# One load of the decoder weights over 128 partitions, gathers issued step by step, and a split of the last pair of chunks: an AdaLN and FFN kernel on one core

## The reference, cut to what matters

```python
# layer 0: a conditioned input, then a top-2 mixture of 8 experts
U   = mu @ W_dec + b_dec            # (128, 64) @ (64, 129 * 30): per sequence a 128 x 30 matrix and 30 offsets
t   = x @ U[:, :128*30] + U[:, 128*30:]   # 30 numbers per token
x0  = t @ V                         # then gate (softmax of the top 2 of 8), experts: gelu(x0 W1 + b1) W2 + b2
x   = x + ffn0(x0)
# layer 1: layer norms, table rows gathered by token id, an integrating MLP, then a ternary FFN
x   = x + ffn1(cond(x, ids, states))
# ffn1: h = silu(a1 x) * (a2 x); h = gelu(h1 h); h = gelu(h2 h); w3 h
```

## Time and profile before

| | us |
|---|---|
| median of 3 runs | 443.49 |
| lowest and highest of 3 runs | 441.01, 443.49 |
| the profiled execution, its own time | 443.04 |
| its span, first to last instruction | 441.2 |
| mean granted TensorE clock in it | 0.978 |

### The profile page before, as it was taken

How to read it: one execution, slowest core, us unless ns; L and a number is a source line. 1 busy time by engine, 2 the same in 40 slices (tenths; PEclk the granted TensorE clock), 3 DMA queues, 4 the chain that set the end, 5 groups by cost and what they waited for, 6 DMA issues and landing times.

```text
span 441.2 us, 5719 instructions
## 1 busy us (share of the span) xinstructions
PE 416.0 (94%) x1804; PEld 272.6 (62%) x1804; DVE 315.6 (72%) x651; ACT 290.7 (66%) x515; POOL 142.8 (32%) x129
## 2 busy tenths in 40 slices
PE   4888998999999999999999999999999997999994
PEld 2856544554656765677567665776577646687773
DVE  2889998887985776766886577596784687656542
ACT  1568775797937766497647763975678455776563
POOL 3016896663631650273028261317211012010000
PEclk9799996999999999999999999999999998999999
DMA  8975564473352352532315245035501100000000
GB/s 242 364 293 161 179 174 119 112 229 68 104 155 51 71 163 97 118 99 73 111 40 159 75 116 150 0 70 181 134 3 49 46 3 0 1 0 25 0 25 27
DMA packets 29961, 45.08 MB, mean 102 GB/s; under 512 B 3461, under 2 KB 22378, under 8 KB 29418
## 3 DMA queue, kind: packets, MB, share of 16 engines
q1 hardware_dynamic: 25440, 32.33, 25.7%
q0 software_dynamic: 3584, 10.49, 7.1%
q10 hardware_dynamic: 906, 1.87, 1.5%
HBM read 40.67 MB, written 4.03 MB: 101 GB/s over the span
## 4 chain that ended last, share of the span: by engine, by line
PE 79%; DVE 8%; ACT 5%; issue 3%; DMA 2%; POOL 2%; another core or an unknown queue 1%; ACTq 0%; POOLq 0%; DVEq 0%
PE bank L644 23%; PE bank L746 20%; PE bank L692 7%; PE bank L636 6%; PE bank L782 6%; PE bank L731 5%; PE bank L823 2%; PE bank L660 2%; DMA muT<-cond_512T_in 2%; PE bank L699 2%; PE bank L771 2%; POOL rstd L1446 1%; ACT mG L890 1%; ACT YN L895 1%
## 5 line engine op out<-in xcount | busy, mean ns | idle before, releaser
L644 PE MATMUL bank<-mG,W 128*128 128x512 f32 x256 | 121.3, 604 | 0.1
L890 ACT ACTIVATE mG<-bank,keepP 128x512 f32<-128x512 f32 x128 | 85.3, 685 | 32.2 <-PE bank L636 30.2
L1446 POOL TENSOR_TENSOR rstd<-ve,mhalf 128x4 f32<-128x4 f32 x24 | 34.0, 1419 | 173.0 <-DVE ve L1196 172.1
L1181 DVE TENSOR_TENSOR mG<-mG,gwbs 128x1024 f32<-128x1024 f32 x64 | 77.1, 1220 | 8.8 <-ACT mG L890 4.4
L644 PEld LDWEIGHTS bank<-mG,W 128*128 128x128 f32 x256 | 48.4, 194 | 44.2 <-issue 39.9
L636 PE MATMUL bank<-ts,A 96*128 96x512 f32 x128 | 66.8, 553 | 1.3 <-ACT mG L890 1.1
L955 ACT ACTIVATE G<-bank,keepP 128x512 f32<-128x512 f32 x48 | 32.8, 696 | 25.4 <-PE bank L746 20.1
L1427 POOL DMA_INDIRECT gp<-pgb_in,ixall x32 | 36.8, 1149 | 27.4 <-DVE norms L1233 17.7
L1430 POOL DMA_INDIRECT gcm<-ctm,ixcm x32 | 36.5, 1140 | 9.8 <-issue 9.8
L746 PE MATMUL bank<-hA_h,h1w_h 128*128 128x512 f32 x96 | 38.9, 405 | 0.0
L746 PE MATMUL bank<-hA_l,h1w_h 128*128 128x512 f32 x96 | 38.6, 402 | 0.0
(11 more groups left out here) (241 smaller groups left out, 804.3 us busy)
## 6 DMA issues: line engine op xcount, KB each, us to landing
gwbs<-gate_w SPq DMA_DIRECT2D x32, 512.0 KB
keep<-xT_in SPq DMA_DIRECT2D x8, 256.0 KB, 5.8
outT<-keep SPq DMA_DIRECT2D x8, 256.0 KB, 2.0
t_split<-tsS SPq DMA_DIRECT2D x7, 192.0 KB
ts<-t_split SPq DMA_DIRECT2D x7, 192.0 KB
W1T<-W1T_in SPq DMA_DIRECT2D x1, 1024.0 KB, 9.4
W<-W2T_in SPq DMA_DIRECT2D x1, 1024.0 KB, 13.8
hs<-h1T_in SPq DMA_DIRECT2D x1, 1024.0 KB, 6.5
```

Source lines behind the costliest of these rows:

```text
L644: mm = pe.matmul(OACC[:, :], W2[:, e * HC + c, :], mG[n % NMG][:, c, :], start=False, stop=(e == E - 1 and c == HC - 1))
L890: act.activation(mG[e % NMG][:, c % HC, :], HM[n % 2][:, :], ACT.Gelu, bias=b1c[:, c:c + 1]).then_inc(m_gelu, 1)
L1181: dve.tensor_tensor(mine, mine, gate.unsqueeze(1).broadcast_to([P, HC, TT, P]), ALU.mult).then_inc(m_q, 1)
L1446: step(pool.tensor_tensor(rstd[:, n, :], ve[:, n, :], mhalf[:, :], ALU.pow))
```

## The change

Three things are changed. First, `W_dec` is loaded by one transfer from SP's queue into `Wd`, over all 128 partitions: its source is seen as two halves h of columns (outermost), 64 rows m and 1920 numbers c. The lower partitions now carry features 0 to 63. The 30 last columns, `wd_u`, are a transfer of their own from ACT's queue, into a place in `gap`; `ld_wd` still counts four transfers. ACT issues `muT` first, then `wd_u`, `bdec`, `V`, `keepP`, `earlyP` and `bdec_u`. The last piece of `Wp` goes from DVE to ACT, and `sq_()` with the two products behind it is moved on DVE from ahead of the additions to behind the copies of G8, just ahead of `tb0`. POOL's two memsets count one each on `wp_zero`, and all wait for 2. Second, the step `tab` of POOL becomes four steps `tab0` to `tab3`, each with the waits of `tab` ahead of its two indirect transfers; in `ORDER` the four follow one another where `tab` was. Third, in the last FFN chunks 10 and 11 (the last two ahead of the last product) get their high and low parts one at a time.

```diff
-        Wd = sb("Wd", [P, KR * (DH + 1)], stack=early)
+        Wd = sb("Wd", [P, KR * DH], stack=early)
...
-        bdec_u = gap[0:KR, KA + KR:KA + KR + 1]
+        wd_u = gap[0:MU, KA + KR:KA + 2 * KR]
+        bdec_u = gap[0:KR, KA + 2 * KR:KA + 2 * KR + 1]
...
-        PIECES = ("v", "v", "v", "a", "v", "a", "v", "v")
+        PIECES = ("v", "v", "v", "a", "v", "a", "v", "a")
...
+        def alone(j, k):
+
+            return j is TAIL["p"] and k >= 3 * FC - 2
+
         def tail_lo(eng, j, k):
 
-            eng.wait_ge(p_lo[j.s], j.n * (FC + 4) + (k + 1 if k < FC else FC + (k - FC) // 2 + 1))
+            eng.wait_ge(p_lo[j.s], k + 1 if k < FC else FC + (k - FC) // 2 + 1 + (alone(j, k) and k % 2))
...
-                    "fgp9 fhp8 fgp10 fgp11 fhp10"),
+                    "fgp9 fhp8 fgp10 fgp11 fhp10 fhp11"),
...
-                    "flp6 -for flp8 flp10 fop"),
+                    "flp6 -for flp8 flp10 flp11 fop"),
...
-                (0, "tcl0 tcl1 tcl2 srt ix tcl3 tab tcl4 tcl5 rt0 tcl6 tcl7 rt1"),
+                (0, "tcl0 tcl1 tcl2 srt ix tcl3 tab0 tab1 tab2 tab3 tcl4 tcl5 rt0 tcl6 tcl7 rt1"),
...
-            load(Wd[0:MU, :], A["W_dec"][:, KR * DH:KR * (D + 1)], ld_wd)
+            load(Wd[:, :], A["W_dec"][:, 0:KR * D].rearrange("m (h c) -> h m c", h=2), ld_wd)
...
-            load(Wd[MU:P, 0:KR * DH], A["W_dec"][:, 0:KR * DH], ld_wd)
             for at in (0, MU):
                 load(muT[at:at + MU, :], A["cond_512T"], ld_wd)
+            load(wd_u, A["W_dec"][:, KR * D:KR * (D + 1)], ld_wd)
+            load(bdec, A["b_dec"][:, 0:KR * D].rearrange("o (i k) -> (o i) k", k=KR), ld_bd)
             load(Vk[:, :], A["V"], ld_v)
             load(keepP[:, :], A["keepP"], ld_v)
-            load(bdec, A["b_dec"][:, 0:KR * D].rearrange("o (i k) -> (o i) k", k=KR), ld_bd)
...
-            sq_()
-            step(dve.tensor_scalar(hs1[:, :], fsc[:, 0:FC], 0.5, None, ALU.mult))
-            dve.tensor_tensor(cs12[:, :], hs1[:, :], fsc[:, FC:2 * FC], ALU.mult)
...
             ins.then_inc(g8_ready, 1)
+            sq_()
+            step(dve.tensor_scalar(hs1[:, :], fsc[:, 0:FC], 0.5, None, ALU.mult))
+            dve.tensor_tensor(cs12[:, :], hs1[:, :], fsc[:, FC:2 * FC], ALU.mult)
             run(steps, ORDER["DVE"])
...
-            def tables(b):
+            def tables(b, t):
...
-                for t in range(TT):
-                    j = b * TT + t
+                j = b * TT + t
```

More of the change, by code:

```diff
@@ L164, in build @@
         Wp = hs[:, 0:KR * D].rearrange("m (k i) -> m k i", k=KR)
-        wd = [Wd[0:MU, :].rearrange("m (i k) -> m k i", k=KR), Wd[MU:P, 0:KR * DH].rearrange("m (i k) -> m k i", k=KR)]
-        wd_u = Wd[0:MU, KR * DH:KR * (DH + 1)]
-        turned_wd = [Wp[0:MU, :, DH:D], Wp[MU:P, :, 0:DH]]
+        halves = (slice(0, MU), slice(0, DH)), (slice(MU, P), slice(DH, D))
+        wd = [Wd[rows, :].rearrange("m (i k) -> m k i", k=KR) for rows, _ in halves]
+        turned_wd = [Wp[rows, :, cols] for rows, cols in halves]
         warmA = sb("warmA", [2, P], stack=early)
@@ L1003, in fh_tail @@
                     return
-                act.wait_ge(p_g[j.s], j.n * 2 * FC + k - FC + 2)
+                w = 1 if alone(j, k) else 2
+                act.wait_ge(p_g[j.s], k - FC + w)
                 dst = hB if k < 2 * FC else hC
-                act.activation(dst[0][:, c:c + 2, j.cols], j.G[:, c:c + 2, j.cols], ACT.Copy).then_inc(p_hi[j.s], 1)
+                act.activation(dst[0][:, c:c + w, j.cols], j.G[:, c:c + w, j.cols], ACT.Copy).then_inc(p_hi[j.s], 1)
             def low_check(n):
@@ L1075, in _ @@
             act.wait_ge(ld_wd, 64)
-            act.wait_ge(wp_zero, 1)
+            act.wait_ge(wp_zero, 2)
             for q in range(8):
@@ L1079, in _ @@
                     mine = slice(4 * q, min(4 * q + 4, KR))
-                    act.activation(turned_wd[1][:, mine, :], wd[1][:, mine, :], ACT.Copy)
-                    act.activation(turned_wd[0][:, mine, :], wd[0][:, mine, 0:DH], ACT.Copy).then_inc(wd_act, 1)
+                    act.activation(turned_wd[0][:, mine, :], wd[0][:, mine, :], ACT.Copy)
+                    act.activation(turned_wd[1][:, mine, :], wd[1][:, mine, :], ACT.Copy).then_inc(wd_act, 1)
             load(w12s[:, :], A["w12T"], ld_w[0])
@@ L1288, in fl_tail @@
                 else:
-                    dst, w = (hB if k < 2 * FC else hC), 2
-                    dve.wait_ge(p_hi[j.s], j.n * (FC + 4) + FC + (k - FC) // 2 + 1)
+                    dst, w = (hB if k < 2 * FC else hC), 1 if alone(j, k) else 2
+                    dve.wait_ge(p_hi[j.s], FC + (k - FC) // 2 + 1 + (alone(j, k) and k % 2))
                 dve.tensor_tensor(dst[1][:, c:c + w, j.cols], j.G[:, c:c + w, j.cols], dst[0][:, c:c + w, j.cols].bitcast(F32),
@@ L1378, in _ @@
             dve.wait_ge(ld_wd, 64)
-            dve.wait_ge(wp_zero, 1)
+            dve.wait_ge(wp_zero, 2)
             for q in range(8):
@@ L1382, in _ @@
                     mine = slice(4 * q, min(4 * q + 4, KR))
[L1383 to L1387 removed]
+                    dve.tensor_copy(turned_wd[0][:, mine, :], wd[0][:, mine, :])
+                    dve.tensor_copy(turned_wd[1][:, mine, :], wd[1][:, mine, :]).then_inc(wd_dve, 1)
             for q in range(0, 8, 2):
@@ L1424, in tables @@
                     weights_done(pool, 3)
[L1425 to L1432 removed]
+                j = b * TT + t
+                pool.indirect_dma_start(out=gp[b % 2][:, t, :], out_offset=None, in_=A["pgb"],
+                                        in_offset=bass.IndirectOffsetOnAxis(ap=ixall[:, 0, j:j + 1].bitcast(U32), axis=0))\
+                    .then_inc(gat[b % 2], 16)
+                pool.indirect_dma_start(out=gcm[b % 2][:, t, :], out_offset=None, in_=CT,
+                                        in_offset=bass.IndirectOffsetOnAxis(ap=ixcm[:, j:j + 1].bitcast(U32), axis=0))\
+                    .then_inc(gat[b % 2], 16)
             def tcl(b):
@@ L1462, in _ @@
             steps = {"tab": tables, "tcl": lambda i, b: tcl(b), "ix": lambda i: ixs(), "rt": root, "srt": lambda i: s_root()}
-            pool.memset(Wp[0:MU, :, 0:DH], 0.0)
-            pool.memset(Wp[MU:P, :, DH:D], 0.0).then_inc(wp_zero, 1)
+            pool.memset(Wp[0:MU, :, DH:D], 0.0).then_inc(wp_zero, 1)
+            pool.memset(Wp[MU:P, :, 0:DH], 0.0).then_inc(wp_zero, 1)
+            pool.wait_ge(wp_zero, 2)
             run(steps, ORDER["POOL"])
```

15 lines of the change are left out of this document (1 added, 14 removed), and 7 rows, old and new, of the table ORDER.

## The result

The changed kernel takes 460.82 us (median of 4 runs, 459.34 to 464.56) against 443.49 (441.01 to 443.93) for the kernel before: a ratio of 1.0418, 95% interval 1.0356 to 1.048. It is slower by 17.3 us in the medians. The profiled execution of the changed kernel took 464.56 us with a span of 462.6, the slowest of its runs. The mean granted clock was 0.951 in it, 0.978 in the profiled execution of before.

What follows compares the result with a forecast made beforehand. PE holds 79% of the span, so the change acts at the front, whose delay passes to the end, and at the last split. 443.04 + 11.9 (Wd's load) + 0.2 (moved steps) + 0 (gathers) - 0.65 (end) = 454.5 us, range 449 to 464.

Steps and rivals of the forecast that it cites:

- +4 for POOL: Upper end for the gathers' extra waits on POOL if nothing covers them: 0.6 us a block, 4 us in all.
- +3 for the clock: Range of 3 us either way for a chain wait of unknown cause and stretches at the lower clock.
- a first copy near 23: Sign of being right: DVE's first copy of Wd starts near 23 us, where it was at 11.11.
- the slow engines: Second rival: two engines carry Wd at 14.3 GB/s each, rows waiting in turn; 469.6 us, first copy after 30; chance 0.05.
- Two engines, from the outermost 2: Wd's load at the front: its source has 2 outermost, so only 2 of 16 DMA engines carry it.
- The price of it, +11.9: Front: Wd's load on two engines fills ld_wd at 23.0 instead of 11.1, which costs 11.9 us.
- I take 26.5: Rate in GB/s assumed for each of Wd's two engines, from 16 engines moving 424; gives 18.5 us for 983 kB.
- Late loads behind it: Front: loads queued behind Wd come later, bdec_u being tightest; cost 0, up to 1 us in the range.
- The moved steps: Front: four DVE operations moved to just ahead of tb0 make it late; +0.2 us, with ends 0 and 0.4.
- The gathers: POOL's tab in four steps: same order, added waits already met; cost 0, upper end 4 us in all.
- The end: Last FFN: chunks 10 and 11 split singly, so the last products finish sooner; -0.65 us, ends -0.4 and -0.8.
- The first, 16 engines and 439.6: First rival: Wd's load is spread over 16 engines, release 3 us sooner, 439.6 us; a gain from five engines on; chance 0.13.

Runs made afterwards that it cites:

- laid-out halves: Changed kernel, but the host writes W_dec's two halves one under the other, so one load has 128 rows outermost: 442.85 us, ratio 1.0004.
- all held: Changed kernel, but every load behind Wd, muT and wd_u on both queues is issued only when these have landed: 455.25 us, one run.
- SP held: Changed kernel, but only SP's loads behind Wd wait until Wd, muT and wd_u have landed; ACT's run beside it: 459.43 us, one run.
- ACT held: Changed kernel, but only ACT's loads from bdec on wait until Wd, muT and wd_u have landed; SP's run beside Wd: 466.35 us, one run.
- old loads: Changed kernel with W_dec's loads, ACT's load order, wd_u's place, the pieces and zeroed blocks as before: 442.73 us, ratio 1.0006.
- 8 outermost: Changed kernel, but the one transfer's source has 8 groups of 16 rows outermost, padded by the host: 446.46 us, one run.
- 4 outermost: Changed kernel, but the one transfer's source has 4 groups of 32 rows outermost, padded by the host: 458.70 us, one run.

## Why the prediction was right

The forecast, 454.5 us with 449 to 464, took the right mechanism and the right sign. The median is 6.3 us above it, inside the range, but that it is inside is partly luck. The front alone was late by 19.65 us at tb0, where the forecast had 12.1 and its upper end, +2 for slower shares, +1 for late loads and +0.2 for the moved steps, 15.3. The room came from +4 for POOL and +3 for the clock, and POOL needed none of it. By the prediction's own signs, a first copy near 23 was to show it right and one after 30 was to show the slow engines; it came at 30.18. The steps in turn:

**Two engines, from the outermost 2.** Right, and shown: two loads of the same bytes take the loss away, the laid-out halves in one load too, and alone the transfer keeps 0.12 to 0.13 of the engines busy. The rule of the Trainium skill (DMA: Bandwidth & Descriptors, "Why a DMA increments its semaphore by 16 and not by 1"), that the outermost sizes of both sides set the number, held where the two sides differ, 2 and 128. The Trainium skill's other rule (the same page, "Rules for kernel authors"), one transfer of 128 partitions in place of two of disjoint halves, did not hold for this source: the one transfer released the copies at 30.18, the two at 9.47. Where the source has 128 rows outermost, the one transfer came close to the two, 10.22 against 9.47.

**The price of it, +11.9, is the term that was mis-sized; it measured +19.07.** By its parts, the release was put at 23.0 and came at 30.18:

| part of the sum | predicted | measured | from |
|---|---|---|---|
| first row of `Wd` | 2.1 | 2.37 | packets, all held |
| the rows alone | 18.5 | 19.4 | 2.37 to 21.81, all held |
| ACT's loads | 2.0 | 2.9 | 24.72 - 21.81, SP held |
| SP's other loads | 0 | 3.3 | 25.10 - 21.81, ACT held |
| both together | 0 | 1.2 | 29.26 - 21.81, less 2.9 and 3.3 |
| last row to first copy | 0.4 | 0.9 | 30.18 - 29.26 |

The step that failed is "I take 26.5", for the whole of the transfer. SP's other loads did queue behind the 64 long rows of each of the two engines, as the prediction has it (the 16 late rows of `W1T`), and so I priced them at nothing. But their parts on the other 14 engines ran meanwhile (so they did not wait on all 16, as the prediction thought they might), and the rows of `Wd` slowed with them: with SP's loads alone beside them (ACT held) the rows of `Wd` that start from 4 to 9 take 401 ns in the mean, and the rows of `W1T` on the other engines 430. In the changed kernel it is 432 and 450, and the stage of 4 to 9 has 261 GB/s with a share of 0.98, some 17 GB/s for each engine. It is about as slow as the stretch of 4 to 6 before (229 GB/s). I had put that one down to the two half loads with their 64 partitions each and expected it to go with them. It stayed, and rows that fell into it or into its like of 21 to 24 took 423 to 476 ns in place of 292. Alone, an engine has its 26 to 27 GB/s. Why all rows are slow while 16 engines are busy in these stretches, and not in others (424 GB/s in the earlier trace rows), no run here shows.

The terms of ACT's loads and of the completion were short by 0.9 and 0.5. The 0.4 for the completion came from no row; from the last row's end to the first copy it is 0.33 with all held, 0.42 with SP's held, 1.00 with ACT's held and 0.92 with none held.

**Late loads behind it, 0 with 1 in the range.** Right for their users: ACT's additions wait for PE (1.09 at 34.98 above), no longer for `b_dec` as in the earlier trace rows, and nothing on the chain up to tb0 waits for SP's late loads.

**The moved steps, +0.2 with 0 to 0.4.** Low: +0.54 in the changed kernel and with the old loads alike, above the upper end. The four operations run one after the other between the `G` copies and tb0, and tb0 starts right behind the last. With the small gaps between them they fill 0.94 us, from 42.61 to 43.55, where 0.40 of idle lay before. The prediction summed their 0.80 of the earlier trace rows, and then took half of what was over without a row for it. Whether the 0.54 reaches the end of the kernel can't be told from the old-loads kernel's ratio of 1.0006.

**The gathers, 0.** Right: POOL's wait for DVE is 174.3 against 172.1.

**The end, -0.65 with -0.4 to -0.8.** The mechanism is right, the size is -0.96, beyond the larger of the two. The two copies of the last chunk alone take 0.53 and 0.70, not 0.62 and 0.74.

**The sum again,** with what the front and the end measured: 443.04 + 19.65 - 0.96 = 461.7, 0.2% from the median of 460.82. The profiled execution has 464.56. Its granted clock was lower than in before's in the blocks. The same work lies about 20 us later in it, so the stage of 100 to 150 stands against 80 to 130 of before (after, then before):

```profile
100.00:150.00 50.00, 48.34 (x167) 27.03 (x166) 40.41 (x98) 38.53 (x75) 28.40 (x25) 0.97 0.54 142
```

```profile
80.00:130.00 50.00, 48.33 (x171) 26.95 (x170) 41.13 (x95) 39.55 (x76) 27.68 (x25) 1.00 0.49 137
```

DVE's 64 products of `mG` with the gates say when the time was lost: the first is 19.5 us later than before's, the 17th to the 46th are 21.7 to 21.8 later and the others behind them 20.7 to 21.7. Ahead of the 17th, at 120.0, lie two stretches of 3.4 us at a granted clock of 0.50, at 92.9 and 106.6, that before's execution does not have. The three other timed runs, with mean granted clocks of 0.956 to 0.961 instead of 0.951, took 459.34 to 461.01, below the 461.7. So the 2.9 us between 461.7 and 464.56 are no cost of the change that the times show.

**The rivals.** The first, 16 engines and 439.6, is refuted by the same rows: 0.16 of the engines' time from 14 to 18, and 30.18. Its price would have been too good as well. With the load spread, the release came at 10.22, not near 8, for `wd_u` took the place of `Wd`, and the time was 442.85; only with `wd_u` out of that wait did it come at 8.75. Its reckoning that five engines would be enough for a gain is wrong too: with 8 outermost the release is at 15.28, behind the 11.11 of before, since the rate of 26.5 for each engine, taken from one stretch, did not hold for them. The second, two engines at 14.3 GB/s and 469.6, had the release after 30 as its mark, and the release is at 30.18: that mark was badly chosen. The engines alone kept 26 to 27 GB/s. What slowed them was the traffic beside them, since without it they had that rate, and not that each row waits for the one before.

## What to carry to other kernels

Before two transfers become one, write down the outermost dimension of both sides: here a view with 2 outermost cost 19 us for 983 kB, and the same rows laid out one under the other cost none of it. Price a transfer on few engines twice, alone and beside everything that the other engines will move meanwhile; the second was 27 us where the first was 19.4. And when a wait is for a sum of loads, ask which of them is late once the big one is fast: here it was 7.5 KB, and they belong under a semaphore of their own.

## What was not expected of the hardware

- Loads queued behind a transfer on two engines are split by it: 14 engines had started their parts of `W1T` by 9.1 us, two did after 28, and the load landed 31.0 us after its issue.
- The number of engines does not divide the time. For 2, 4 and 8 outermost the rows of 7680 B took 373, 653 and 668 ns in the mean beside other loads; alone, 304 for 2 and 384 for 4. The cause is open.
- A transfer on two engines holds up the sequencer that issues others behind it. SP's issues of `b2f` took 4.76 us for three (0.95 with the old loads), and the load of `W` left at 28.84 instead of 11.59. It happens with more engines too: the same load left at 27.56 with 4 outermost and at 15.77 with 8, where it took 3.49 to issue. With SP's loads held until `Wd` was in, the three of `b2f` took 0.95 again.
- The granted clock was 0.50 (the 1.2 GHz level) from 14 to 18 and beyond, after PE's warming products had ended, and still from 31 to 34 with the first products running. In the kernel before it was 0.50 from 12 to 15, with the first products running, too, and the mean over the 40 first is 0.71 in both (6.51 and 6.48 us). Up to tb0 the wait cost its own length and no more.
